# A macaron layer on one core: rows laid out by partition, two end blocks on ScalarE and GpSimd, slot products between the halves of a chunk, expert numbers packed

## The reference

```python
x = x + 0.5 * ffn(layernorm(x), ...)
x = x + attention(layernorm(x), ...)     # 16 heads of 128, causal
x = x + 0.5 * ffn(layernorm(x), ...)     # same weights as the first
# ffn, for 1024 tokens x of width 256:
shared = (silu(g) * u) @ shared_down_w.T           # width 704
shared = sigmoid(x @ shared_gate_w.T) * shared
probs = softmax(x @ gate_w.T)                      # 8 experts
top_w, top_i = top_k(probs, 2);  top_w /= top_w.sum()
out = sum over the two chosen experts e of top_w * ((silu(ge) * ue) @ w2[e].T) + shared
```

## Time and profile before

| what | us |
|---|---|
| three runs: median (lowest to highest) | 521.12 (520.67 to 521.65) |
| the profiled execution's own time | 521.58 |
| its span in the profile | 519.8 |
| busy of PE, DVE, ACT, POOL in the span | 503.7, 348.1, 276.0, 279.2 |
| clock granted to PE, mean of the span (1 is 2.4 GHz) | 0.996 |

### The profile page before, as it was taken

How to read it: one execution, slowest core, us unless ns; L and a number is a source line. 1 busy time by engine, 2 the same in 40 slices (tenths; PEclk the granted TensorE clock), 3 DMA queues, 4 the chain that set the end, 5 groups by cost and what they waited for, 6 DMA issues and landing times.

```text
span 519.8 us, 10686 instructions
## 1 busy us (share of the span) xinstructions
PE 503.7 (97%) x3329; PEld 452.5 (87%) x3329; DVE 348.1 (67%) x922; ACT 276.0 (53%) x815; POOL 279.2 (54%) x371
## 2 busy tenths in 40 slices
PE   8999999998999999999999999999999999999994
PEld 4787999887798998999988989999988788899983
DVE  5788766489464775856846847658558578866646
ACT  3983666624462654645636736546445465466540
POOL 1896777732861671652734716716542242677740
PEclk9999999999999999999999999999999999999998
DMA  8951333252002001010010010010001230233335
GB/s 274 388 191 52 105 106 106 103 164 70 21 0 62 2 22 61 20 61 0 20 61 0 20 61 15 14 52 20 0 2 42 81 123 0 83 102 106 108 123 193
DMA packets 20128, 39.41 MB, mean 76 GB/s; under 512 B 2944, under 2 KB 10496, under 8 KB 20096
## 3 DMA queue, kind: packets, MB, share of 16 engines
q1 hardware_dynamic: 15680, 26.92, 15.6%
q0 software_dynamic: 4416, 12.06, 7.1%
HBM read 29.80 MB, written 9.18 MB: 75 GB/s over the span
## 4 chain that ended last, share of the span: by engine, by line
PE 88%; DVE 7%; DMA 1%; issue 1%; POOL 1%; ACT 1%; SPq 0%; POOLq 0%; DVEq 0%
PE bank L183 21%; PE bank L185 20%; PE bank L184 20%; PE bank L1708 5%; PE bank L1720 4%; PE bank L1707 3%; PE bank L1749 3%; PE bank L1144 2%; DVE x_res L975 2%; PE bank L1020 2%; PE bank L189 1%; PE bank L1747 1%; PE bank L190 1%; DMA xn<-y_by_token 1%; PE bank L1192 1%
## 5 line engine op out<-in xcount | busy, mean ns | idle before, releaser
L1452 POOL TENSOR_TENSOR s_a<-s_a,rr_a 128x128 f32<-128x128 f32 x64 | 25.7, 401 | 133.6 <-DVE rr_a L1569 132.8
L1502 ACT ACTIVATE s_a<-s_a,mn_a 128x128 f32<-128x128 f32 (+1 forms) x128 | 57.1, 458 | 18.6 <-DVE mn_a L1563 18.4
L183 PE MATMUL bank<-xT_h,area_h 128*128 128x512 f32 x124 | 51.3, 414 | 0.0
L1495 ACT ACTIVATE qk_a<-bank,bias_a 128x512 f32<-128x512 f32 x32 | 22.0, 688 | 51.2 <-PE bank L185 48.5
L185 PE MATMUL bank<-xT_h,area_l 128*128 128x512 f32 x124 | 48.6, 392 | 0.0
L184 PE MATMUL bank<-xT_l,area_h 128*128 128x512 f32 x124 | 48.5, 391 | 0.0
L571 POOL DMA_INDIRECT xn<-x_normed,tok_i_f x38 | 37.2, 979 | 20.1 <-issue 9.8
L1517 ACT ACTIVATE area_h<-bank,bias_a 128x256 fp32r<-128x256 f32 x64 | 29.0, 478 | 29.3 <-PE bank L1749 28.6
L1551 DVE TENSOR_SCALAR qk_a<-bank,bias_a 128x512 f32<-128x512 f32 x32 | 24.0, 750 | 29.9 <-PE bank L185 29.9
L1563 DVE TENSOR_REDUCE mn_a<-s_a 128x1 f32<-128x128 f32 (+1 forms) x128 | 39.2, 347 | 2.2
L1559 DVE SCALAR_TENSOR_TENSOR s_a<-bank,cst 128x384 f32<-128x384 f32 x64 | 35.2, 549 | 8.1 <-PE bank L1708 8.0
(11 more groups left out here) (210 smaller groups left out, 1712.1 us busy)
## 6 DMA issues: line engine op xcount, KB each, us to landing
area<-in_wqkv SPq DMA_DIRECT2D x8, 768.0 KB, 4.2
area_r<-in_w SPq DMA_DIRECT2D x16, 256.0 KB, 4.3
w_r<-in_w SPq DMA_DIRECT2D x8, 352.0 KB, 7.4
x_normed<-xn SPq DMA_DIRECT2D x4, 512.0 KB, 4.9
area<-in_wo SPq DMA_DIRECT2D x8, 256.0 KB, 2.6
xn<-y_by_token SPq DMA_DIRECT2D x8, 256.0 KB, 4.0
x_res<-in_x_in SPq DMA_DIRECT2D x4, 256.0 KB, 4.4
wgu_r<-in_wgu SPq DMA_DIRECT2D x4, 256.0 KB, 7.0
```

What stands on the lines that cost most here:

```text
L183: pe.matmul(psum, lhs[0], rhs[0], start=first, stop=False)
L1502: act.activation(s[b][:, cols], s[b][:, cols], ACT.Exp, bias=mn[:, b, t:t + 1], scale=-1.0, accum_out=rs[:, b, t:t + 1]).then_inc(s_e, 1)
```

## The change

- `x_normed` and `y_by_token` are laid out by partition: the 8 rows of a partition stand together (16 in `y_by_token`, two per token), with the area for empty slots behind them. A load of y for one block is 128 pieces of 2 KB instead of 256 of 1 KB. The arithmetic of `tokens` follows, with as many instructions as before.
- PE's slot products stand between the two halves of chunk 7.
- `tile_experts` packs the experts' numbers, three bits each, into three words with one more product on DVE. PE loads three registers once and takes each tile's number by a shift and a mask (`unpack`) instead of a load.
- In the last block, j = 5 and j = 7 (`alone`) are scaled by ACT and added by POOL. The other six (`paired`) stay on DVE. Their loads are issued in the order 0, 1, 2, 3, 5, 7, 4, 6; ACT issues the stores of 5 and 7. A store of the first block of a pair waits for one addition less than before.

```diff
-VOID = -(-NM // NT) * NT
+ROWS = TOP_K * NT
+PACK = 8
+WORDS = -(-NM // PACK)
+BITS = 3
...
-    c[:, C_P] = r
-    c[:, C_J:C_J + TOP_K * NT] = VOID + np.arange(TOP_K * NT)
-    c[:, C_VOID:C_VOID + NM] = P * np.arange(NM) + r[:, None]
+    c[:, C_P] = r - 1
+    choice, block = np.divmod(np.arange(TOP_K * NT), NT)
+    c[:, C_J:C_J + TOP_K * NT] = ROWS + TOP_K * block + choice
+    c[:, C_VOID:C_VOID + NM] = TOP_K * TOK + P * np.arange(NM) + r[:, None]
...
-        yd = nc.dram_tensor("y_by_token", (VOID * P + TOP_K * TOK, D), FP32, kind="Internal").ap()
+        yd = nc.dram_tensor("y_by_token", (TOP_K * TOK + NM * P, D), FP32, kind="Internal").ap()
...
+                alone = [] if after else [NT // 2 + 1, NT - 1]
+                paired = [j for j in range(NT) if j not in alone]
...
-                            sp.dma_start(xd.rearrange("(j p) d -> p j d", p=P)[:, j:j + HT, :],
+                            sp.dma_start(xd.rearrange("(p j) d -> p j d", p=P)[:, j:j + HT, :],
...
-                    for j in range(NT):
-                        sp.dma_start(y_buf(j), yd[VOID * P:, :].rearrange("(t j p) d -> j p t d", t=TOP_K, p=P)[j]
+                    for j in range(NT) if after else (*range(NT // 2), *alone, *paired[NT // 2:]):
+                        sp.dma_start(y_buf(j), yd[0:TOP_K * TOK, :].rearrange("(p j t) d -> j p t d", t=TOP_K, p=P)[j]
...
-                        for j in range(NT):
-
-                            sp.wait_ge(s_add, pair_added(j))
-                            sp.wait_ge(s_dnv, j + 1)
+                        for j in paired:
+                            sp.wait_ge(s_add, pair_added(j) - 1 + paired.index(j) % 2)
+                            sp.wait_ge(s_dnv, paired.index(j) + 1)
...
+                    for at, j in enumerate(alone):
+                        for k, part in enumerate((hs[at][:, 0:D], y_buf(j)[:, 0, :], y_buf(j)[:, 1, :])):
+                            pool.wait_ge(s_scaled, 3 * at + k + 1)
+                            if k:
+                                pool.wait_ge(s_lone, 3 * at + k)
+                            pool.tensor_tensor(x_res[:, j, :], x_res[:, j, :], part, ALU.add).then_inc(s_lone, 1)
...
+                    for at, j in enumerate(alone):
+                        act.wait_ge(s_dn, sums(j))
+                        act.activation(hs[at][:, 0:D], out_bank(j), ACT.Identity,
+                                       scale=gates_r[:, 1, j:j + 1]).then_inc(s_scaled, 1)
+                        act.wait_ge(s_y[Y_BUF[j]], y_count(j))
+                        for t, w in enumerate((gates_r[:, 0, j:j + 1], cw2[:, j:j + 1])):
+                            act.activation(y_buf(j)[:, t, :], y_buf(j)[:, t, :], ACT.Identity,
+                                           scale=w).then_inc(s_scaled, 1)
+                    for at, j in enumerate(alone):
+                        act.wait_ge(s_lone, 3 * (at + 1))
+                        act.dma_start(out[:, j, :], x_res[:, j, :]).then_inc(s_out, 16)
...
+                        link(dve.tensor_tensor(tile_cmp[0:1, :, :], tile_cmp[0:1, :, :],
+                                               cst[0:1, C_POW:C_POW + PACK * WORDS].unsqueeze(2).to_broadcast(every),
+                                               ALU.mult))
...
+                            dve.tensor_reduce(words[0:1, :], in_words.rearrange("p (a b) -> p a b", a=WORDS),
+                                              op=ALU.add, axis=AX.X).then_inc(s_expert, 1)
...
-                        link(dve.tensor_tensor(tok_f, bank[5][:, 0:NM], tok_f, ALU.add))
-                        link(dve.scalar_tensor_tensor(place[:, :], code, float(P), tok_f, ALU.mult, ALU.add))
-                        dve.tensor_scalar(tok_i[:, :], place[:, :], TOK - 1, None,
+                        link(dve.tensor_tensor(tok_f, code, tok_f, ALU.add))
+                        link(dve.scalar_tensor_tensor(place[:, :], bank[5][:, 0:NM], float(ROWS), tok_f,
+                                                      ALU.mult, ALU.add))
+                        dve.tensor_scalar(tok_i[:, :], place[:, :], 1, TOK - 1, ALU.logical_shift_right,
                                           ALU.bitwise_and).then_inc(s_tok, 1)
...
                         add(h)
+                        if h == 1 and not after:
+                            shared_out(paired[NT // 2])
...
-                    for j in (NT // 2, NT // 2 + 1):
-                        shared_out(j)
                     if after:
+                        for j in (NT // 2, NT // 2 + 1):
+                            shared_out(j)
                         norm_apply(dve, after, 0, 1)
+                    else:
+                        shared_out(paired[-1])
                     dve.wait_ge(s_dnv, NT // 2 + 2)
                     add(NT // 2)
                     add(NT // 2 + 1)
-                    add(NT - 2)
+                    if after:
+                        add(NT - 2)
...
-                    else:
-                        add(NT - 1)
-                        last_outs()
...
-                    shared_up(7)
-                    slot_tokens()
+                    shared_up(7, slot_tokens)
...
+                    def unpack(m):
+                        pe.reg_alu(e_up, e_words[m // PACK], BITS * (m % PACK), ALU.logical_shift_right)
+                        pe.reg_alu(e_up, e_up, NE - 1, ALU.bitwise_and)
...
                     def next_experts(m):
                         pe.reg_mov(e_down, e_turn)
                         pe.reg_mov(e_turn, e_up)
-                        pe.reg_load(e_up, tile_e[0:1, bass.ds(m, 1)])
+                        unpack(m)
...
-                        for reg in (e_up, e_turn):
-                            pe.reg_load(reg, tile_e[0:1, 0:1])
+                        for w in range(WORDS):
+                            pe.reg_load(e_words[w], words[0:1, w:w + 1])
+                        unpack(0)
+                        pe.reg_mov(e_turn, e_up)
```

More of the change, by code:

```diff
@@ L61 @@
 R1 = 12
+PACK = 8
+WORDS = -(-NM // PACK)
+BITS = 3
+assert 1 << BITS == NE and BITS * PACK <= 24
 C_ID = 0
@@ L68 @@
 C_MI = C_LT + NE * NE
-C_MP = C_MI + NM
-C_P = C_MP + NM
+C_MP = C_MI + PACK * WORDS
+C_POW = C_MP + NM
+C_P = C_POW + PACK * WORDS
 C_J = C_P + 1
@@ L334, in ffn @@
                     in_bank(at_tiles + 2 * NE + a * TOP_K * NT, [TOP_K * NT], FP32 if a == 0 else I32) for a in range(4)]
-                tile_cmp = wg_tile[0:1, 0:NM * (NE - 1)].rearrange("p (a b) -> p a b", b=NE - 1)
-                tile_e = sb("tile_e", [1, NM], I32)
+                in_words = wg_tile[0:1, 0:PACK * WORDS * (NE - 1)]
+                tile_cmp = in_words.rearrange("p (a b) -> p a b", b=NE - 1)
+                words = sb("words", [1, WORDS], I32)
                 gates = sb("gates", [P, 2, NT])
@@ L381, in ffn @@
                 s_out = None if first else sem("s_out")
+                alone = [] if after else [NT // 2 + 1, NT - 1]
+                paired = [j for j in range(NT) if j not in alone]
+                s_scaled = sem("s_scaled") if alone else None
+                s_lone = sem("s_lone") if alone else None
                 def ring_uses(m, depth):
@@ L479, in pair_added @@
                 def pair_added(j):
-                    return 2 * TOP_K * (j // 2 + 1)
+                    return 2 * TOP_K * (paired.index(j) // 2 + 1)
                 def attention_high(act, t):
@@ L825, in tile_experts @@
                         link(dve.tensor_tensor(end[:, :], base[:, :], tiles_of[:, :], ALU.add))
+                        every = [1, PACK * WORDS, NE - 1]
                         link(dve.tensor_tensor(tile_cmp[0:1, :, :],
-                                               cst[0:1, C_MI:C_MI + NM].unsqueeze(2).to_broadcast([1, NM, NE - 1]),
-                                               end[0:1, 0:NE - 1].unsqueeze(1).to_broadcast([1, NM, NE - 1]),
-                                               ALU.is_ge))
-                        with nc.allow_low_precision(reason="a count of at most seven"):
-                            dve.tensor_reduce(tile_e[0:1, :], tile_cmp[0:1, :, :], op=ALU.add,
-                                              axis=AX.X).then_inc(s_expert, 1)
+                                               cst[0:1, C_MI:C_MI + PACK * WORDS].unsqueeze(2).to_broadcast(every),
+                                               end[0:1, 0:NE - 1].unsqueeze(1).to_broadcast(every), ALU.is_ge))
+                        link(dve.tensor_tensor(tile_cmp[0:1, :, :], tile_cmp[0:1, :, :],
+                                               cst[0:1, C_POW:C_POW + PACK * WORDS].unsqueeze(2).to_broadcast(every),
+                                               ALU.mult))
+                        with nc.allow_low_precision(reason="eight counts of at most seven, three bits each"):
+                            dve.tensor_reduce(words[0:1, :], in_words.rearrange("p (a b) -> p a b", a=WORDS),
+                                              op=ALU.add, axis=AX.X).then_inc(s_expert, 1)
```

(6 more changed lines are left out.)

5 lines of the change are left out of this document (3 added, 2 removed).

## The result

The changed kernel takes 524.24 us (median of 4 runs, 523.56 to 524.78), the kernel before 521.13 beside it: ratio 1.0051, 95% interval [1.0038, 1.0064]. It is slower, where 518.8 was forecast. Its profiled execution took 523.56, its span is 521.4, and the clock was 0.993 of full speed.

A forecast was written before the change was run, and what follows sets the result against it. PE was taken to bound the kernel (88% of the span), with DVE's additions queued behind it at the end. First block 0.0, second -0.7, tail -1.3, store -0.3: -2.3, a median of 518.8, range 517.3 to 520.8.

The forecast's parts named there:

- Blocks 5 and 7 off DVE: Last block's end: two blocks' additions move to ACT and POOL, ending 2.9 after PE instead of 4.2: -1.3.
- A: Tile loop: one more PE register instruction per tile shows in some 40 steps, +4.0, giving 523.2, slower; chance 0.09.
- Tail, 2.9 after PE: After PE's last product: ACT's scaling, then three dependent POOL additions of 0.72, together 2.9 instead of 4.2.
- Last store, 2.8: End of the kernel: the last store, alone on ACT's queue, takes 2.8 instead of about 3.1: -0.3.
- Slots, +0.33 a block: Between chunk 7's halves: PE waits for token_hot, costing +0.33 in each block, while POOL's train starts 1.03 earlier.
- Earlier train, -0.86: Second block's tile loop: earlier gathers and scatters free ACT's buffers, and two PE steps of 2.43 become 2.00: -0.86.
- The -0.1 for the first block: First block's tile loop: one ACT wait reaches PE by about 0.1, and the earlier train removes it.
- Words, -0.2 a block: First down product of each block: shift and mask replace an exposed register load on PE, -0.2 per block.
- in the steady steps nothing shows: Tile loop: register loads cost PE's steady steps nothing, since 2.00 is the sum of the products' own intervals.
- PE together: Slots, train and words summed on PE: first block 0.0, second block -0.7.
- Rows, 0: Loads of y and store of x_normed, laid out by partition in larger pieces: costed at nothing.
- Rival C: Last block's loads: pieces 16 KB apart land more slowly, DVE ends after POOL, giving 519.3; chance 0.10.

The follow-up runs named there:

- e9: The changed kernel plus one GpSimd DRAIN in the last block, between its last scatter and its first addition of the tail: 518.29, 0.9933 of the kernel before.
- e7: The changed kernel, but only block 4 goes to ScalarE and GpSimd, loaded first; VectorE adds the other seven in another order: 0.9963 of the kernel before.
- e10: e9 with block 7's two y terms scaled and added first and its shared result last: 0.9948 of the kernel before.
- e4: The kernel before with only the slot products moved between the halves of chunk 7: 0.9996 of the kernel before, 0.9982 when run again.
- e1_again: The changed kernel without GpSimd's part at the end, all eight blocks' additions on VectorE: 519.47, 0.9955 of the kernel before.
- e5: The kernel before with only the experts' numbers packed in three words, shift and mask on PE: 0.9982 of the kernel before, 0.9980 when run again.
- e8: e1_again with VectorE's last additions reordered so that only block 7's shared result needs PE's last product: 519.09, 0.9947 of the kernel before.

## Why the prediction was wrong

**The step that failed is "Blocks 5 and 7 off DVE"**, in what it left out, not in its sum. It followed the tail to the last store and stopped there. What an engine does after its program was taken as nothing for all of them. GpSimd's closing DRAIN takes 7.6 after its last instruction, as in a program that does little else than issue 92 indirect DMAs, and the change moved that last instruction from 501.7 to 513.6, from under 18 us of cover to the end. Without it the span would have ended about 0.2 after SP's DRAIN at 515.6, so it cost 5.6; with it paid early the time falls by 5.9 (524.17 to 518.29). The row was in the trace of before, on a line that no instruction of the kernel's text has. None of the rivals had it; A reached 523.2 by another mechanism, which the 2.00 steps refute: that it lies near the measured time is chance. e9 is the kernel that the forecast described, and it gains more than forecast, 3.5 instead of 2.3, by other terms: PE ends 1.68 earlier (510.32) instead of 0.7, and POOL's last addition is over 3.72 after PE instead of 2.9.

The other terms:

- *Tail, 2.9 after PE:* 3.05 measured, additions 0.72 and 1.59 for two. Right. That DVE would be slowed beside POOL was not foreseen. It costs nothing in the changed kernel. In e7 and e10 it took part of the expected gain; no run separates it from e7's DRAIN and e10's wait for a load. What the share is worth is -1.2 by medians against -1.6 forecast with the store.
- *Last store, 2.8:* 2.1 (waits of SP's queue, above), hidden here.
- *Slots, +0.33 a block:* in the first block the tiles start 0.34 later (50.10 against the earlier trace rows), as forecast, with the wait on DVE moved along. In the second the price is the same, though the tiles start at 447.00 in both traces: PE reaches chunk 7 0.32 earlier, by the first block's gain. Its half ends with the product that starts at 439.12, the next could start 0.23 later, at 439.35, and the slots start at 439.67: 0.32 lost. (The row's 0.16 counts from the modelled end of an overlapping product.)
- *Earlier train, -0.86:* right in size; the mechanism only in part. The two steps of 2.43 and 2.47 are 2.00, and the first gather comes 1.36 earlier, 1.04 against the start of chunk 7. But ACT still waits 0.63 for a scatter, where the prediction wanted none over 0.3, and the slots alone (e4) leave a step of 2.58, slots, words and rows without GpSimd's share (e1_again) one of 2.46. The -0.1 for the first block isn't the train's: its long steps go with the words (e5) and stay without them (e4).
- *Words, -0.2 a block:* the step with the first down product fell from 2.59 to 2.36 and 2.38, as forecast. That "in the steady steps nothing shows" was wrong. The loads also stretched steps by 0.03 to 0.22: 0.5 in the first block, 0.2 in the second. This was in the trace of before as well, in steps that the prediction didn't list.
- *PE together:* the first block gains 0.4 net (+0.34 - 0.23 - 0.5), of which 0.32 arrive at chunk 7 of the second. There +0.32 for the slots uses it up, then -0.21 - 0.86 - 0.18 make 1.24 up to the last turn (489.94 against 491.18), and 0.21 more fall in the last two tiles. The last product comes 1.46 earlier where 0.7 was forecast: the words were mis-sized, the train not.
- *Rows, 0:* not measurable within the change. The whole trace has 16543 packets instead of 20128. Rival C's mechanism exists, since the later loads land more slowly (above), but it doesn't set the end here: DVE waits only 0.24 for a load at the end and is done before POOL.

**The best version** measured is e9: the whole change and one DRAIN on GpSimd in the 6.7 when it has nothing to do. It takes 518.29, 0.9933 [0.9920, 0.9946] of the kernel before; the intervals of e8 and e10 overlap with it.

## What to carry to other kernels

The end of the span is the end of the last engine's closing, not of the last store: before giving late work to an engine that was done early, read what its queue does after its last instruction. If GpSimd has issued indirect DMAs, let it drain while others work. And where a loop should be periodic, list every step: single steps of 2.1 among steps of 2.0 are a cost with a cause.

## What the runs showed of the hardware

- GpSimd's DRAIN ends 0.1 us after its last operation without indirect DMAs, 0.2 with one, 7.6 with 92, landed or not; paid once, it isn't paid again (0.1 in e9).
- VectorE's scalar_tensor_tensor on 128x256 fp32, all in SBUF: 0.48 alone, 0.72 to 0.96 when it starts beside a GpSimd tensor_tensor; GpSimd's own additions took 0.72 to 0.96 there. One of VectorE's with an input in PSUM (L796 at 509.19) kept 0.47 beside GpSimd. The Trainium skill's page GPSIMD Engine Reference, "Specifications", has GpSimd share its SBUF interfaces with VectorE and names VectorE's instructions with two SBUF inputs among those that contend; the rows above agree.
- The Trainium skill's page VectorE: DVE Perf Modes, "The DRAIN you can't avoid", takes the DRAINs around a kernel as constants of about 12 ns on all five engines. SP's 7 ns fits; GpSimd's 8357 ns doesn't, and the measurement decides. DVE's 1757 ns is another case: it starts at 511.3, while DVE still adds, and ends with DVE's last addition (513.00) to within 0.1.
- A register load on TensorE's queue takes 0.30 and mostly hides; in 46 steps with one each, some were stretched by up to 0.22; with six loads in all, ahead of the tiles, none was but for stalls behind scatters.
- Loads of 256 KB in pieces of 2 KB, 16 KB apart in DRAM: the last ones of eight took 6.5 to 7.7 from issue to landing in the first block, those in pieces of 1 KB without such gaps 5.5 to 6.1. The first four took 3.5 to 4.2 (medians) either way.
